# Graph rows for the neighbour table prepared one pass ahead in a pipelined four-layer graph kernel

## The chip, the cores and the metric

The kernel runs on one core of one Trainium2 chip. The metric is the time of one execution on the device in microseconds (us). For the kernel before it is the median of three runs.

## What is computed

Eight graphs of 1024 nodes with 128 features each, and an integer adjacency matrix of 1024 x 1024 for each graph. Four residual layers follow one another:

```
x = x + gnn0(adj, layernorm(x))      # for each node: maximum over the normalised rows of its
                                     # first 25 neighbours, concatenated with its own, matmul, relu
x = x + ffn0(layernorm(x))           # 8 experts, top 2, hidden 512, gelu
x = x + attention(layernorm(x), adj) # 8 heads of 16, masked by the adjacency
x = x + ffn1(layernorm(x))           # router of 64, 6 experts of 128, top 2, three layers, relu
```

The first layer needs rows of arbitrary neighbours: `feats = X[idx]` with X the normalised rows of the whole graph, and then the maximum over them.

## The kernel before

The work of four graphs overlaps. A pass `g` does the attention and the second expert layer of graph g (`att`), prepares the attention of graph g+1 (`unit`), does the graph layer's matmul and the first expert layer of graph g+2 (`near`), and gathers the neighbours of graph g+3 (`load`). The passes -3, -2 and -1 fill this pipeline, passes 0 to 4 are one hardware loop over the same code, and passes 5, 6 and 7 drain it (L586 to L602).

For each pass `planned` (L113) writes down chains of steps and what each step waits for; `schedule` (L250) puts the steps into one list, by a table of assumed durations (`COURSE`). Every engine walks that one list in order and does its own part of each step. So within an engine the order is fixed by the list, and engines wait for one another by semaphores. The steps that matter here:

- `load_x` (SP, L713): the rows of graph g+3 into `xn0`, 512 KB. `lnv(0)` (VectorE, L831 to L836) takes mean and variance, `sq(0)` (ScalarE, L1212) the root, `ln(0)` (VectorE, L850, L852) normalises in place. `store_x` (SP, L723) writes `xn0` to `table` in device memory.
- `load_adj(t)` (SP, L728) brings one of eight row tiles of the adjacency, `deg(t)` (ScalarE, L1196, L1199) counts degrees, `class(t)` (TensorE L1308, ScalarE L1204, L1207) classes the tile, `find(t)` (VectorE, L870 to L886) searches the slot indices.
- The gathers (POOL, L794): 8, 16 or 25 indirect DMAs per tile from `table` into `G`. POOL waits once in a pass for the stored table, then for `find(t)` and for `pmax(t-2)` of each tile. `pmax(t)` (VectorE, L902 to L919) takes the maximum.
- In the next pass `gT` transposes `xn0` and the maxima, `gnn` multiplies, `gnn_add` (VectorE, L930, L933) adds to `res_n`, which `load_res` (SP, L720) has loaded.
- `qT` (ScalarE) copies the transposed rows of the attention input to `XB`; `qk(1)` and `v` (the projections, TensorE) read it. After `v` nothing reads `XB` until the next pass.
- `stack(0)` and `stack(1)` (SP, L748): twelve loads each of query and key parts. `load_mask(t)` (SP, L732), `mask(t)` and `s(t,h)` (TensorE L1408, VectorE L1124): score maxima, 64 a pass.
- `st`, `av` (TensorE L1431, L1434, L1445, ScalarE L1258): attention, in the first third of a pass. `up0`, `down0` (L1386, L1396) and ScalarE's GELU (L1251): first expert layer. `u1`, `u2`, `y1`: second expert layer, after `t1`, `r1`, `lg1` (its router).

SP's queue carries all loads and stores but the gathers. It, too, is walked in order: an SP instruction that waits holds up every transfer behind it.

Of the kernel before, what the change touches and what calls it, by code (L numbers as in the profile page):

```python
# [24 lines left out]
P = 128  # L25
# [87 lines left out]
def planned(att, unit, near, load):  # L113

    p = Plan()
# [4 lines left out]
    if att:  # L120
# [15 lines left out]
        p.gate(("lnv", 3), ("ln", 0) if load else None)  # L136
# [20 lines left out]

    if load:
        p.chain([("load_x",), ("lnv", 0), ("sq", 0), ("ln", 0), ("store_x",)])
        p.gate(("load_x",), ("gT",) if near else None)  # L160
        p.threads.append([("pmax", t) for t in range(TILES)])
        p.threads.append([("gather", t) for t in range(TILES)])
        p.chain([k for t in range(TILES) for k in (("load_adj", t), ("deg", t), ("class", t), ("find", t))])
        p.gate(("find", 0), ("shift",))
        for t in range(TILES):
            p.gate(("gather", t), ("find", t), ("store_x",), ("pmax", t - 2) if t >= 2 else None)
            p.gate(("pmax", t), ("gather", t))
        if not near:
            p.threads.append([("load_w",)])
            p.gate(("load_w",), ("load_adj", 0))  # L170
# [79 lines left out]
def schedule(att, unit, near, load):  # L250


    p = planned(att, unit, near, load)
# [61 lines left out]
def signals(step):  # L315
# [21 lines left out]
    if k == "load_x":  # L337
        return [("xin", step, 16)]
    if k == "store_x":
        return [("tab", step, 16)]  # L340
# [74 lines left out]
class Pass:  # L415


    def __init__(self, before, att, unit, near, load):
        self.att, self.unit, self.near, self.load = att, unit, near, load
        self.steps = schedule(att, unit, near, load)  # L420
# [26 lines left out]
def graph_kernel(nc, x, adj, gW, gb, Wg, bg, W1, b1, W2, b2, Wq, Wk, Wv, Wo, bo,  # L447
                 rw1, rb1, rw2, rb2, ew1, eb1, ew2, eb2, ew3, eb3, out):
    ctx = ExitStack()
    with ctx:  # L450
# [3 lines left out]
        def sem(name):  # L454
# [90 lines left out]
        rden = sb("rden", [P, HTILES, GH])  # L545
        XF = mask[:, TILES - 2:TILES, :].rearrange("p a n -> p (a n)").bitcast(F32)
# [26 lines left out]
            "took": "residual_taken", "resx": "residual_loaded", "tab": "table_stored",  # L573
# [12 lines left out]
        for g in range(-3, GRAPHS):  # L586
            parts_of = (g >= 0, 0 <= g + 1 < GRAPHS, 0 <= g + 2 < GRAPHS, g + 3 < GRAPHS)
            if g > 0 and all(parts_of):
                continue
            passes.append((g, Pass(state, *parts_of)))  # L590
            loops = GRAPHS - 3 if all(parts_of) else 1
            state = passes[-1][1].after(loops)

        def over_passes(eng, body):

            for g, ps in passes:
                if g == 0:
                    with eng.Fori(0, GRAPHS - 3) as b:
                        body(ps, b, b)
                else:  # L600
                    body(ps, 0, g)
# [101 lines left out]
        def _(sp):  # L703
# [3 lines left out]
            def body(ps, turn, b):  # L707
                for step in ps.steps:
                    kind = step[0]
                    if kind == "load_x":  # L710
                        if ps.near:
                            sp.wait_ge(*is_taken(ps, turn, ("xn", 1)))
                        sp.dma_start(xn0[:, :, :], x_v[b + 3, :, :, :]).then_inc(S["xin"], 16)  # L713
# [7 lines left out]
                    elif kind == "store_x":  # L721
                        sp.wait_ge(*at(ps, turn, "xn0", ("ln", 0)))
                        sp.dma_start(table[0:NODES, :].rearrange("(t p) c -> p t c", p=P),  # L723
                                     xn0[:, :, :]).then_inc(S["tab"], 16)
# [39 lines left out]
        def _(pool):  # L764
# [54 lines left out]
        def _(dve):  # L819
# [5 lines left out]
            def moments(ps, turn, i):  # L825
# [3 lines left out]
                src, own = (xn0, res_n, res_b, res_f)[i], (1, 0, 0, 1)[i]  # L829
# [8 lines left out]
            def norm(ps, turn, step):  # L838

                i = step[1]  # L840
                src, dst = ((xn0, xn0), (res_n, xn), (res_b, xn), (res_f, xn))[i]
# [339 lines left out]
        def _(act):  # L1181
# [7 lines left out]
            def body(ps, turn, b):  # L1189
                for step in ps.steps:  # L1190
# [26 lines left out]
                    elif kind == "qT":  # L1217
                        for hf in range(2):
# [67 lines left out]
        def _(pe):  # L1286
# [15 lines left out]
            def body(ps, turn, b):  # L1302
                for step in ps.steps:
# [11 lines left out]
                    elif kind == "gT":  # L1315

                        pe.wait_ge(*at(ps, turn, "xn0"))
# [213 lines left out]
```

## Time and profile before

| what | us |
|---|---|
| median of 3 runs (lowest, highest) | 3047.97 (3043.27, 3052.67) |
| the profiled execution | 3052.26 |
| its span, from the first to the last instruction | 3050.2 |
| TensorE (PE) busy | 2532.1, 83% |
| VectorE (DVE) busy | 1840.7, 60% |
| ScalarE (ACT) busy | 1340.0, 44% |
| POOL busy | 865.5, 28% |
| mean granted TensorE clock | 0.932 |

The engine shares are averages over passes that are limited by different things, so they are read pass by pass. A busy TensorE isn't necessarily at its peak: the ends of its matmuls are modelled. "issue" in a list of waits is time in which an engine waited for nothing that the profile shows.

### The profile page before, as it was taken

To read this page: it belongs to the slowest core of one execution; us is meant where nothing else is said; L and a number is where in the kernel's file an instruction comes from. 1 tells how busy PE (TensorE), PEld (TensorE's weight loads), DVE (VectorE), ACT (ScalarE), POOL (GpSimd) and SP (SyncE) were. 2 spreads that over 40 slices of the span, in tenths; PEclk is the share of its full clock that TensorE was granted. 3 is DMA by queue.
4 is the path that set the end of the run, shared out by engine and by line. 5 is a ranking of instruction groups with operands and counts; after the bars stand their busy time and mean duration, and the time that the engine had idled before them with its cause. 6 is when DMAs were issued, how large, how long until landed. Compare 5 with 4: busy or idle time off the path is not lost.

```text
span 3050.2 us, 48344 instructions
## 1 busy us (share of the span) xinstructions
PE 2532.1 (83%) x16137; PEld 1511.7 (50%) x16137; DVE 1840.7 (60%) x5404; ACT 1340.0 (44%) x1993; POOL 865.5 (28%) x917
## 2 busy tenths in 40 slices
PE   0039559888799989998899889998899999997796
PEld 0026436444466445654466445654566556644253
DVE  5345467874686558764686557865686188318603
ACT  1024224166434653366435653366425553552163
POOL 4737536307500472017400572007500000000000
PEclk9989869889899999999999999999999999998697
DMA  6626666327401372118411483117411120021000
GB/s 148 81 45 82 79 110 82 52 67 107 72 29 44 78 117 37 43 56 111 65 42 41 83 105 41 43 56 128 49 42 36 25 46 28 29 42 36 22 1 7
DMA packets 107565, 183.69 MB, mean 60 GB/s; under 512 B 21471, under 2 KB 57724, under 8 KB 107260
## 3 DMA queue, kind: packets, MB, share of 16 engines
q0 software_dynamic: 25344, 51.96, 19.0%
q1 hardware_dynamic: 81916, 128.08, 15.3%
q8 instruction: 141, 2.31, 0.3%
q14 instruction: 164, 1.34, 0.1%
HBM read 158.59 MB, written 20.97 MB: 59 GB/s over the span
## 4 chain that ended last, share of the span: by engine, by line
PE 37%; DVE 34%; issue 13%; DVEq 6%; ACT 4%; DMA 3%; SPq 2%; ACTq 0%
DVE tmp L1124 14%; PE PY L1396 7%; PE PH L1386 7%; PE PA L1431 5%; PE PA L1434 5%; PE PY L1445 4%; DVE G L902 2%; DMA adj_sb<-in_adj 2%; DVE res_f L1026 2%; PE PA L1408 2%; DVEq L822 2%; ACT HB L1258 2%; DVE res_n L1026 2%; SPq L748 2%; DVE score L870 2%
## 5 line engine op out<-in xcount | busy, mean ns | idle before, releaser
L794 POOL DMA_INDIRECT G<-table,slot_idx x792 | 839.0, 1059 | 262.6 <-issue 258.7
L1124 DVE CUSTOM_DVE_ANT_0 tmp<-PA,mask 128x1024 bf16<-128x1024 f32 x512 | 626.9, 1225 | 34.8 <-issue 34.8
L1258 ACT ACTIVATE HB<-PA 128x1024 f32<-128x1024 f32 x512 | 498.1, 1022 | 328.2 <-PE PA L1434 327.0
L1251 ACT ACTIVATE HB<-PH,bias_T 128x512 f32<-128x512 f32 x512 | 351.4, 687 | 613.3 <-PE PH L1386 613.1
L1386 PE MATMUL PH<-XT,W_sb 128*128 128x512 f32 x1024 | 521.1, 625 | 33.4 <-ACT HB L1251 16.6
L1396 PEld LDWEIGHTS PY<-W_sb,HB 128*128 128x128 f32 x4096 | 504.5, 192 | 68.9 <-issue 38.5
L1396 PE MATMUL PY<-W_sb,HB 128*128 128x128 f32 x4096 | 509.4, 276 | 2.5 <-DVE res_n L1026 2.5
L1431 PE MATMUL PA<-QS,KS 99*128 99x512 bf16 x1024 | 407.1, 398 | 12.0 <-ACT HB L1258 7.6
L1434 PE MATMUL PA<-identb,mask 128*128 128x128 bf16 x4096 | 410.6, 224 | 0.0
L1434 PEld LDWEIGHTS PA<-identb,mask 128*128 128x128 bf16 x4096 | 328.2, 100 | 135.9 <-issue 19.2
L1408 PE MATMUL PA<-KS,QS 96*128 96x512 bf16 x1024 | 335.1, 412 | 54.2 <-DVE MX L1124 46.8
L675 POOL TENSOR_TENSOR pool_pad<-pool_pad 1x1 f32<-1x1 f32 x112 | 23.5, 219 | 1063.6 <-DVE slot_idx L882 912.4
L1386 PEld LDWEIGHTS PH<-XT,W_sb 128*128 128x128 f32 x1024 | 178.4, 196 | 207.8 <-ACT HB L1251 107.6
L1445 PE MATMUL PY<-HB,VS 128*32 128x512 f32 x2048 | 274.7, 608 | 1.9 <-ACT HB L1258 1.9
L671 DVE MEMSET dve_pad<- 1x1 f32 x669 | 39.5, 59 | 363.0 <-DMA G<-table,slot_idx 151.4
L1279 ACT ACTIVATE parts<-PH,bias_T 128x512 f32<-128x512 f32 x192 | 131.9, 687 | 256.0 <-PE PH L1494 161.8
L1408 PEld LDWEIGHTS PA<-KS,QS 96*128 96x128 bf16 x1024 | 88.7, 100 | 285.2 <-DVE MX L1124 140.2
L1026 DVE SCALAR_TENSOR_TENSOR res_n<-PY,wts,res_n 128x128 f32<-128x128 f32 x512 | 144.3, 344 | 119.7 <-PE PY L1396 108.8
L1431 PEld LDWEIGHTS PA<-QS,KS 99*128 99x128 bf16 x1024 | 102.1, 100 | 177.7 <-ACT HB L1258 136.5
L1290 PE MATMUL PH<-ident,xn 128*128 128x128 f32 x256 | 44.5, 320 | 138.3 <-DVE bias_T L1076 67.3
L902 DVE TENSOR_TENSOR G<-G 128x256 f32<-128x256 f32 (+5 forms) x154 | 110.9, 720 | 59.7 <-issue 52.9
L1153 DVE COPY tmp<-PY 128x512 f32<-128x512 f32 x32 | 22.1, 692 | 205.7 <-PE PY L1445 203.5
(163 smaller groups left out, 2388.3 us busy)
## 6 DMA issues: line engine op xcount, KB each, us to landing
adj_sb<-in_adj SPq DMA_DIRECT2D x64, 512.0 KB
adjm<-in_adj SPq DMA_DIRECT2D x64, 512.0 KB
G<-table,slot_idx POOLq DMA_INDIRECT x792
parts_dram<-parts SPq DMA_DIRECT2D x16, 768.0 KB, 3.5
QS<-parts_dram SPq DMA_DIRECT2D x96, 128.0 KB, 5.6
KS<-parts_dram SPq DMA_DIRECT2D x96, 128.0 KB, 7.9
xn<-in_x SPq DMA_DIRECT2D x8, 512.0 KB, 5.3
table<-xn SPq DMA_DIRECT2D x8, 512.0 KB, 4.3
```

Source lines behind the costliest of these rows:

```text
L794: pool.indirect_dma_start(G[:, t % 2, s, :], None, table, bass.IndirectOffsetOnAxis(slot_idx[:, t, s:s + 1], axis=0), bounds_check=ROWS - ...
L902: settle(dve.tensor_tensor(g[:, 0:even, :], g[:, 0:even, :], g[:, even:2 * even, :], ALU.max))
L1026: ins = dve.scalar_tensor_tensor(out=res[:, t, :], in0=psum(ps, key)[:, tt * C:(tt + 1) * C], scalar=wts[layer][:, layer * TILES + t, e:e ...
L1124: ins = dve.tensor_tensor_reduce(out=junk, in0=psum(ps, step)[:, :], in1=mask[:, t, :], scale=1.0, scalar=LOWEST, op0=ALU.add, op1=ALU.max ...
L1251: act.activation(HB[:, i % 2, c, :], psum(ps, step)[:, :], ACT.Gelu, bias=bias_T[:, e * HC + c:e * HC + c + 1]).then_inc(*emptied(ps, step))
L1258: act.activation(HB[:, kc % 2, 2 * pr:2 * pr + 2, :], psum(ps, key)[:, :].rearrange("p (h q) -> p h q", h=2), ACT.Exp, scale=float(D) ** - ...
L1386: pe.matmul(psum(ps, step)[:, :], W1_sb[:, e, c * P:(c + 1) * P], XT[:, half[hf]], start=True, stop=True).then_inc(*filled(ps, step))
L1396: ins = pe.matmul(psum(ps, key)[:, tt * C:(tt + 1) * C], HB[:, i % 2, c, tt * P:(tt + 1) * P], W2_sb[:, e, c, :], start=(c == 0), stop=(c ...
L1408: ins = pe.matmul(psum(ps, step)[:, half[hf]], QS[0:SROWS, h, t * P:(t + 1) * P], KS[0:SROWS, h, half[hf]], start=True, stop=True)
L1431: pe.matmul(o, KS[0:SROWS + PARTS, h, kc * P:(kc + 1) * P], QS[0:SROWS + PARTS, h, half[qh]], start=True, stop=False)
L1434: ins = pe.matmul(o[:, qt * P:(qt + 1) * P], mask[:, qh * HTILES + qt, kc * P:(kc + 1) * P], identb[:, :], start=False, stop=(qt == HTILES ...
L1445: ins = pe.matmul(psum(ps, key)[32 * hh:32 * hh + 32, :], VS[:, kc, (D + 1) * (g * GH + hh):(D + 1) * (g * GH + hh) + 32], HB[:, kc % 2, h ...
```

## The change

A fifth part of a pass, `ahead`, does `load_x`, `lnv(0)`, `sq(0)`, `ln(0)` and `store_x` for graph g+4. The pipeline gets one more pass at its start (-4), and the loop has four passes (0 to 3); pass 4 becomes code of its own. The rows are loaded and normalised in `XB` (under the name `XR`), so `load_x` waits for the projection `v`, and the store waits until the current graph's last maximum is taken and the table has been read. A new step `again` (SP) reads the normalised rows of graph g+3 back from the table into `xn0`, where `load_x` stood. POOL now waits for the table of the preceding pass.

```diff
+    if ahead:
+        p.chain([("load_x",), ("lnv", 0), ("sq", 0), ("ln", 0), ("store_x",)])
+        p.gate(("load_x",), ("v",) if unit else None)
+        p.gate(("lnv", 0), ("ln", 3) if att else None, ("ln", 1) if near else None)
+        p.gate(("store_x",), ("pmax", TILES - 1) if load else None, ("again",) if load else None)
+
     if load:
-        p.chain([("load_x",), ("lnv", 0), ("sq", 0), ("ln", 0), ("store_x",)])
-        p.gate(("load_x",), ("gT",) if near else None)
+        p.threads.append([("again",)])
+        p.gate(("again",), ("gT",) if near else None)
...
         for t in range(TILES):
-            p.gate(("gather", t), ("find", t), ("store_x",), ("pmax", t - 2) if t >= 2 else None)
+            p.gate(("gather", t), ("find", t), ("pmax", t - 2) if t >= 2 else None)
...
-        for g in range(-3, GRAPHS):
-            parts_of = (g >= 0, 0 <= g + 1 < GRAPHS, 0 <= g + 2 < GRAPHS, g + 3 < GRAPHS)
+        for g in range(-4, GRAPHS):
+            parts_of = (g >= 0, 0 <= g + 1 < GRAPHS, 0 <= g + 2 < GRAPHS, 0 <= g + 3 < GRAPHS, g + 4 < GRAPHS)
...
                     if kind == "load_x":
-                        if ps.near:
-                            sp.wait_ge(*is_taken(ps, turn, ("xn", 1)))
-                        sp.dma_start(xn0[:, :, :], x_v[b + 3, :, :, :]).then_inc(S["xin"], 16)
+                        if ps.unit:
+                            sp.wait_ge(*is_taken(ps, turn, ("v", 1)))
+                        sp.dma_start(XR, x_v[b + 4, :, :, :]).then_inc(S["xin"], 16)
+                    elif kind == "again":
+                        stored = settled(sp, at(ps, turn, "tab"))
+                        if ps.near:
+                            seen = settled(sp, is_taken(ps, turn, ("xn", 1)))
+                            sp.wait_ge(*seen)
+                        sp.wait_ge(*stored)
+                        sp.dma_start(xn0[:, :, :], table[0:NODES, :].rearrange("(t p) c -> p t c", p=P)).then_inc(S["xrow"], 16)
...
                 if ps.load:
                     pool.drain()
-                    pool.wait_ge(*at(ps, turn, "tab", ("store_x",)))
+                    pool.wait_ge(*at(ps, turn, "tab"))
...
                     elif kind == "qT":
+                        act.wait_ge(*at(ps, turn, "tab"))
```

In `COURSE` the assumed duration of `load_x` goes from 7 to 14, and `again` gets 6.

The steps of the list move accordingly. SP's queue in the loop pass, from the second half of the stack loads to the adjacency tile 6, of the kernel before:

```order
L748 DMA QS<-parts_dram 16x4x1024 x6
L748 DMA KS<-parts_dram 16x4x1024 x6
L731 REGISTER_ALU
L732 ISA
L732 DMA adjm<-in_adj 128x1024
L727 REGISTER_ALU
L728 ISA
L728 DMA adj_sb<-in_adj 128x1024
```

and of the change:

```order
L772 DMA QS<-parts_dram 16x4x1024 x6
L772 DMA KS<-parts_dram 16x4x1024 x6
L720 REGISTER_ALU
L721 ISA
L721 DMA XB<-in_x 128x8x128
L755 REGISTER_ALU
L756 ISA
L756 DMA adjm<-in_adj 128x1024
L751 REGISTER_ALU
L752 ISA
L752 DMA adj_sb<-in_adj 128x1024
```

The x load (L721) has come in ahead of the mask's adjacency tile and of adjacency tile 6.

VectorE in the same place of the loop pass, from `ln(3)` to the search `find(6)`, of the kernel before:

```order
L850 RECIPROCAL rstd<-sq 128x8
L852 TENSOR_SCALAR xn<-res_f,mv,rstd 128x128 x8
L1023 REGISTER_ALU
L1026 SCALAR_TENSOR_TENSOR res_n<-PY,wts,res_n 128x128 x4
L866 REGISTER_ALU
L671 MEMSET dve_pad 1x1
L868 TENSOR_LOAD degree_class
```

and of the change:

```order
L874 RECIPROCAL rstd<-sq 128x8
L876 TENSOR_SCALAR xn<-res_f,mv,rstd 128x128 x8
L1047 REGISTER_ALU
L1050 SCALAR_TENSOR_TENSOR res_n<-PY,wts,res_n 128x128 x4
L852 REGISTER_ALU
L855 BN_STATS st<-XB 128x6 x8
L858 BN_AGGR mv<-st 128x2 x8
L860 TENSOR_SCALAR sd<-mv 128x8
L890 REGISTER_ALU
L679 MEMSET dve_pad 1x1
L892 TENSOR_LOAD degree_class
```

`lnv(0)` stands ahead of `find(6)` now; its reciprocal and normalisation (`ln(0)`) stand right behind `find(6)`. Of the score maxima L1124 that VectorE did before the router's `sm`, four come later.

ScalarE behind the hole that the profile shows there, of the change (L1236 is the root `sq(0)` with its table load, L1209 are the copies of `t1`; before, the copies followed the GELU L1251 directly):

```order
L1276 ACTIVATE HB<-PH,bias_T 128x512
L1235 REGISTER_ALU
L1236 ACT_TABLE_LOAD
L1236 ACTIVATE sq<-sd 128x8
L1209 ACTIVATE mask<-PH 128x512
```

The next GELU after it needs its table loaded again; in the attention stage a pair of loads around the root is gone, so a pass has as many loads as before.

## Rows read from the trace of the kernel before

**Rows 1.** The page: its first line.

```profile
span 3050.2 us, 48344 instructions
```

**Rows 2.** Busy time by pass: stretch, length, busy us of each engine, clock, DMA share, GB/s.

```profile
187.00:372.00 185.00, 137.64 (x734) 94.21 (x733) 95.25 (x288) 67.59 (x132) 112.79 (x119) 0.86 0.56 69
...
952.00:1290.00 338.00, 308.36 (x2017) 187.71 (x2017) 227.89 (x671) 169.45 (x251) 105.88 (x111) 0.96 0.35 65
```

(The engines are PE, PEld, DVE, ACT and POOL, each with its number of instructions.)

**Rows 3.** Timeline of POOL: its first wait in passes -3, -2 and -1.

```profile
39.17 0.18 POOL L675 TENSOR_TENSOR pool_pad<-pool_pad 1x1 f32<-1x1 f32 x1 [35.60 <-DMA table<-xn]
...
216.38 0.18 POOL L675 TENSOR_TENSOR pool_pad<-pool_pad 1x1 f32<-1x1 f32 x1 [39.84 <-DVE slot_idx L882]
...
421.09 0.18 POOL L675 TENSOR_TENSOR pool_pad<-pool_pad 1x1 f32<-1x1 f32 x1 [58.28 <-DMA table<-xn]
```

**Rows 4.** Waits in pass 1 (952 to 1290): us in total, times, longest.

```profile
POOL pool_pad L675 <- DVE slot_idx L882: 192.6, 1, 192.6
```

**Rows 5.** Busy time by stage of pass 1, columns as in rows 2.

```profile
966.00:1093.00 127.00, 117.22 (x1023) 65.79 (x1024) 72.84 (x222) 89.43 (x126) 53.55 (x54) 0.93 0.45 84
...
1104.00:1124.00 20.00, 10.52 (x50) 6.11 (x49) 8.74 (x36) 9.55 (x17) 10.78 (x15) 0.85 0.72 109
...
1166.00:1259.00 93.00, 90.88 (x456) 56.96 (x455) 80.08 (x212) 31.12 (x46) 2.80 (x3) 1.00 0.16 41
1259.00:1296.00 37.00, 36.65 (x200) 24.47 (x199) 26.20 (x70) 12.12 (x18) 0.00 (x0) 1.00 0.10 35
```

**Rows 6.** Pass 1: a link of the chain that ended last, then TensorE's timeline.

```profile
1104.48 15.23 DMA adj_sb<-in_adj
...
1121.49 0.19 PE L1308 MATMUL PH<-excess,ones 128*1 128x2 f32 x2 [7.67 <-ACT excess L1199]
```

**Rows 7.** The same wait in pass 0, and ScalarE's wait for adjacency in pass 3.

```profile
PE PH L1308 <- ACT excess L1199: 10.7, 1, 10.7
...
  DMA adj_sb<-in_adj: 1.0, 1
```

**Rows 8.** Timeline of VectorE, pass -3: the first statistics.

```profile
16.52 1.64 DVE L831 BATCH_NORM_STATS2 st<-xn 128x6 f32<-128x128 f32 x8
```

**Rows 9.** Timeline of VectorE, pass 1: `lnv(0)`, the next statistics, `ln(0)`.

```profile
982.83 1.65 DVE L831 BATCH_NORM_STATS2 st<-xn 128x6 f32<-128x128 f32 x8 [0.16 <-issue]
...
985.54 1.64 DVE L831 BATCH_NORM_STATS2 st<-res_n 128x6 f32<-128x128 f32 x8
...
1001.84 2.14 DVE L852 TENSOR_SCALAR xn<-xn,mv,rstd 128x128 f32<-128x128 f32 x8
```

**Rows 10.** Timeline of ScalarE, pass 1: table load and root of `sq(0)`.

```profile
999.67 1.28 ACT L1212 ACT_TABLE_LOAD   x1
1000.97 0.21 ACT L1212 ACTIVATE sq<-sd 128x8 f32<-128x8 f32 x1
```

**Rows 11.** The page, DMA issues: KB each, median us from issue to landing.

```profile
xn<-in_x SPq DMA_DIRECT2D x8, 512.0 KB, 5.3
table<-xn SPq DMA_DIRECT2D x8, 512.0 KB, 4.3
```

**Rows 12.** SP's timeline, start of pass 0: first and last of four loads, its landing.

```profile
623.56 0.36 SPq L728 DMA_DIRECT2D adj_sb<-in_adj  x1
...
625.46 0.38 SPq L713 DMA_DIRECT2D xn<-in_x  x1
...
DMA to landing us min/median/max: 7.0/7.0/7.0
```

**Rows 13.** Timeline of VectorE: `find(0)` of pass -2, pass -2's end, `gnn_add` of pass -1.

```profile
205.27 1.23 DVE L870 SCALAR_TENSOR_TENSOR score<-adj_sb,countdown 128x1024 f16<-128x1024 int32 x1 [0.59 <-issue]
...
369.36 0.06 DVE L919 MEMSET dve_pad<- 1x1 f32 x1 [0.29 <-issue]
...
375.87 0.69 DVE L930 TENSOR_TENSOR tmp<-PH,gb_b 128x512 f32<-128x512 f32 x1 [1.31 <-PE PH L1332]
```

**Rows 14.** Timeline of TensorE: its first instruction in pass 1.

```profile
966.48 0.65 PE L1290 MATMUL PH<-ident,xn 128*128 128x128 f32 x4 [2.28 <-issue]
```

More of the change, by code:

```diff
@@ L110, in chain, with planned @@
         return line
-def planned(att, unit, near, load):
+def planned(att, unit, near, load, ahead):
     p = Plan()
@@ L247, with schedule @@
 LATER = {"y0", "y1", "av", "ctx", "proj", "lg0", "lg1", "wT", "gnn", "b", "qk", "mT"}
-def schedule(att, unit, near, load):
-    p = planned(att, unit, near, load)
+def schedule(att, unit, near, load, ahead):
+    p = planned(att, unit, near, load, ahead)
     heads = [0] * len(p.threads)
@@ L415, with __init__ @@
 class Pass:
-    def __init__(self, before, att, unit, near, load):
-        self.att, self.unit, self.near, self.load = att, unit, near, load
-        self.steps = schedule(att, unit, near, load)
+    def __init__(self, before, att, unit, near, load, ahead):
+        self.att, self.unit, self.near, self.load, self.ahead = att, unit, near, load, ahead
+        self.steps = schedule(att, unit, near, load, ahead)
         self.start = dict(before)
@@ L572, in graph_kernel @@
             "xn": "normed_ready", "x1": "gnn_done", "xin": "x_loaded",
[L573 removed]
+            "took": "residual_taken", "xrow": "normed_input_back", "resx": "residual_loaded", "tab": "table_stored",
             "adj": "adjacency_loaded", "adjf": "adjacency_used",
@@ L590, in graph_kernel @@
             passes.append((g, Pass(state, *parts_of)))
-            loops = GRAPHS - 3 if all(parts_of) else 1
+            loops = GRAPHS - 4 if all(parts_of) else 1
             state = passes[-1][1].after(loops)
@@ L597, in over_passes @@
                 if g == 0:
-                    with eng.Fori(0, GRAPHS - 3) as b:
+                    with eng.Fori(0, GRAPHS - 4) as b:
                         body(ps, b, b)
@@ L721, in body @@
                     elif kind == "store_x":
-                        sp.wait_ge(*at(ps, turn, "xn0", ("ln", 0)))
+                        if ps.load:
+                            normed_last = ps.steps.index(("ln", 0)) > ps.steps.index(("pmax", TILES - 1))
+                            again = settled(sp, at(ps, turn, "xrow", ("again",)))
+                            if normed_last:
+                                sp.wait_ge(*at(ps, turn, "xn0", ("ln", 0)))
+                            else:
+                                sp.wait_ge(*at(ps, turn, "aggr", ("pmax", TILES - 1)))
+                            sp.wait_ge(*again)
+                        else:
+                            sp.wait_ge(*at(ps, turn, "xn0", ("ln", 0)))
                         sp.dma_start(table[0:NODES, :].rearrange("(t p) c -> p t c", p=P),
-                                     xn0[:, :, :]).then_inc(S["tab"], 16)
+                                     XR).then_inc(S["tab"], 16)
                     elif kind == "load_adj":
@@ L828, in moments @@
                     dve.wait_ge(*at(ps, turn, "xin", ("load_x",)))
-                src, own = (xn0, res_n, res_b, res_f)[i], (1, 0, 0, 1)[i]
+                src, own = (XR, res_n, res_b, res_f)[i], (1, 0, 0, 1)[i]
                 for t in range(TILES):
```

8 lines of the change are left out of this document (5 added, 3 removed), and 2 rows, old and new, of the table COURSE.

## The prediction

> **What bounds the kernel now.** I read the page first, then busy time by pass, then the waits of one loop pass, then its stages. The span is 3050.2 us [rows 1]. The program is a pipeline of passes: -3 (gathers only), -2, -1, the loop of five passes 0 to 4, and 5 to 7, which gather nothing. Two kinds of pass are bound by different things.
>
> In pass -2 TensorE is busy for 138 of 185 us and POOL, with its gathers, for 113 [rows 2]; its gathers start late, since POOL sat 39.8 us waiting for the first slot indices [rows 3]. Behind the last gather stand two maxima and the next pass, so this pass ends when its gathers do: moving their start moves its end.
>
> In a loop pass TensorE is busy for 308 of 338 us [rows 2], and POOL waits 192.6 us for slot indices [rows 4]: its 106 us of work have room. In the attention stage TensorE is busy 117 of 127 us, VectorE 73, ScalarE 89 [rows 5]. In the late stretch (1166 to 1259) TensorE is busy 90.9 of 93 and VectorE 80: both are nearly full. In the last 37 us VectorE has some 11 to spare. The one hole is between 1104 and 1124, where TensorE works 10.5 of 20 us [rows 5]. There the chain of waits runs through the load of adjacency tile 6: 15.2 us from issue to use, since it stands behind twelve stack loads on SP's queue. ScalarE waits for it, and in order behind that stand the GELUs that TensorE needs; TensorE waits 7.67 us in this pass [rows 6], 10.7 in pass 0, while in pass 3 ScalarE waits for that tile only 1.0 us [rows 7].
>
> Does the table hold the gathers up at all, which the change addresses? Only twice: in pass -3 (released at 39.17) and in pass -1 (421.09); in pass -2, as in the loop, it is the slot indices [rows 3, 4].
>
> **The start (pass -4 new, pass -3).** The table of graph 0 must now be stored before SP goes on. VectorE is free for the first statistics at 16.52 [rows 8]. Statistics take 2.7 us (982.83 to 985.54), the normalisation 2.1 plus a short reciprocal, 2.5 in all [rows 9]; ScalarE's table load and root lie between, 1.28 and 0.21 [rows 10]. The store is issued near 16.5 + 2.7 + 1.5 + 2.5 = 23.2 and lands 4.3 us later [rows 11], at 27.5. Only then do the read-back and adjacency tile 0 go out. Four such loads took 8.9 us (623.56 to 625.46 + 7.0) [rows 12], and one alone 4.3, so each further one costs about 1.5 to 2.2; tile 0 is there near 34. Degree and class take an estimated 3 us (the class matmul runs 1.8 us after a tile has landed, at 1119.7 and 1121.49 [rows 6], and the search another one later). With the search of 11 us (205.27 to 216.38) [rows 3, 13] that gives slot indices near 48 where POOL was released at 39.17: **+9 us**. Bounds 6 and 12.
>
> **Pass -2.** Ahead of the search for tile 0 VectorE did the statistics of the new x (2.7), ln(1) and ln(0) (2.5 each) [rows 9]; now all three come behind it. Gathers start 7.7 us sooner, and the pass ends with them: **-8**. SP is one thing that could spoil it: load_res and adjacency tile 0 now stand behind the store, which waits for the last maximum. Four transfers in 8.9 us [rows 12] arrive just as gnn_add and the search come up, so I count nothing; if the rate is worse, up to +4.
>
> **Pass -1.** The same queue at its start holds store, adjacency, mask adjacency and load_res, where before the middle two had long been loaded. gnn_add started at 375.87; with SP released by the last maximum at 369.4 [rows 13], the four are there near 378.5: **+3**. The x load takes the place of a store of equal size before the same adjacency tile, so it adds nothing here; VectorE's work only changes places. That the gathers may start some 20 us sooner pays nothing: begun at 421 [rows 3] and as long as those of pass -2 (216 to 369), they end near 574, and the pass only near 620 [rows 12].
>
> **The loop, attention stage.** Statistics and normalisation (5.2 us of VectorE), one table store, and on ScalarE a table load for the root plus one back to exp, 2.6 + 0.2 us, go. They lay beside TensorE, which is full here, and VectorE waits for TensorE right after, at the logits. I take **-0.5** in each of five passes (-2.5); bounds 0 and the whole ScalarE piece, 2.8.
>
> **The loop, the hole.** In four passes (0 to 3) the 512 KB x load now stands between the stacks and adjacency tile 6. Its price is not in the trace: at the quiet rate 2.2 us [rows 12], alone to landing 5.3 [rows 11]. The DMA engines are full here and gathers run beside it, so I take 3.5, nearer the middle. It goes straight onto the wait of 10.7, 7.7 and the like [rows 6, 7] in passes 0 to 2, 10.5 in all; in pass 3, with 1.0 of wait, I take 1.5. **+12**. The wait added at issue (for the projection v) is over before the stacks are out.
>
> **The loop, behind the hole.** lnv(0) can run while tile 6 is awaited: free. ln(0), 2.5 us, and the two table switches come after it, on the way to router 1 and the first score maxima; four of the maxima move later. Behind it both engines are near full, but the last 37 us give VectorE 11 to spare [rows 5], and the moved maxima land there, with less expert work left behind them. I take **+1.5** each, +6; bounds 0 and 5.2 + 2.8.
>
> A rule on that: the Trainium skill (ScalarE: Activation LUTs, What ACT_TABLE_LOAD costs) says that a switch takes 1.28 us of load and 1.38 of drain. By that, as an estimate from the page, the pair behind the hole would cost 2.7 us more per pass and the whole change 11 more. The trace has the load at 999.67 and the root at 1000.97 [rows 10]: the load and nothing after it. The rows decide.
>
> **The loop edge.** After each loop pass TensorE waits 2.28 us with nothing to wait for [rows 14]. The loop has four passes now, the fifth being straight code: one edge fewer, **-2**. Pass 4 has no x load at all, which the 4 instead of 5 counts above contain.
>
> **Sum**: 9 - 8 + 3 - 2.5 + 12 + 6 - 2 = +17.5. On the profiled execution's 3052.3 us that is 3069.8; the median of the runs is 4.3 lower, so **3065 us**, 0.6% over it.
>
> **The rivals**, against the median of 3048. A measurement of this kernel tells about 0.3% (9 us) from no change.
>
> *Absorbed (0.27)*: the x load costs 2.2 as in the quiet queue, VectorE's steps fit the slack. 9 - 8 + 3 - 4.5 + 3 x 2.2 = +6: 3054. For it: VectorE idles in the hole too (8.7 busy of 20) [rows 5].
>
> *Faster (0.14)*: ScalarE, not TensorE, ends last in the attention stage, and the moved switches free 2.8 us in each of five passes; tile 6 isn't delayed, since SP's issue of the stacks, not their bytes, sets its arrival. 9 - 8 + 3 - 2 - 14 = -12: 3036. It decides if TensorE's 10 idle us in that stage [rows 5] shrink by more than one per pass. Against it: ScalarE is busy 89 of 127.
>
> *VectorE bound (0.14)*: behind the hole VectorE ends last throughout. Its 5.2, the switches' 2.8 and a load at its full 5.3 add up to 13.3 in four passes: 53 + 4 - 4.5 = +52, 3100. For it: 80 of 93 busy besides the gaps between instructions; against: the slack in the last stretch.
>
> *No earlier gathers (in the forecast, 0.45)*: the change does not do what it says in the loop, because the indices, not the table, start the gathers [rows 4]. That is already counted: it brings nothing there.
>
> **How the numbers follow.** Forecast 0.45, its own range 3055 to 3080 (0.43 of it slower by over 0.3%, 0.02 within). Absorbed 0.27: 0.24 within 0.3%, 0.03 slower. VectorE bound 0.14: slower. Faster 0.14: 0.12 faster by over 0.3%, 0.02 within. That is faster 0.12, same 0.28, slower 0.60. For 8 in 10 the range reaches from 3037, near the faster case's middle, to 3092, which leaves out half of the faster case and most of the VectorE-bound one.
>
> **What would show it.** Pass -3 ends 7 to 11 us later, pass -2 at about the same time as before. POOL's first wait is for slot indices, near 48. In passes 0 to 2 TensorE's wait at the class of tile 6 grows from 8 to 11 us to 11 to 14. The attention stage keeps its length within 1 us. One 2 us wait at a loop edge is gone. I would be wrong if that wait didn't grow, if the attention stage lost 2 us or more, or if the stretch behind the hole grew by more than 4 us per pass.

## The result and the profile after

The changed kernel takes **3083.41 us** (median of 4 runs, 3081.49 to 3089.24) against 3049.95 for the kernel before beside it: ratio 1.0116, 95% interval [1.0094, 1.0138], some 35 us slower by the ratio. The forecast was 3065 (3037 to 3092).

The page of the kernel after: its first line, VectorE's and POOL's busy time, and the two transfers that answer to [rows 11].

```profile
span 3081.0 us, 47928 instructions
...
PE 2529.2 (82%) x16137; PEld 1511.3 (49%) x16137; DVE 1840.1 (60%) x5407; ACT 1339.5 (43%) x1993; POOL 861.5 (28%) x917
...
XB<-in_x SPq DMA_DIRECT2D x8, 512.0 KB, 10.9
table<-XB SPq DMA_DIRECT2D x8, 512.0 KB, 2.9
```

The x load now takes 10.9 us to land instead of 5.3. Where the time went is read from the end of each pass: the moment at which SP issues the first copy of the score maxima (`QS<-mT`). Length of each pass in the two profiled executions, us:

| pass | before, us | after, us | difference | forecast |
|---|---|---|---|---|
| up to the end of -3 | 183.0 | 188.2 | +5.2 | +9 |
| -2 | 186.4 | 180.0 | -6.4 | -8 |
| -1 | 252.0 | 274.5 | **+22.5** | +3 |
| 0, 1, 2, 3 | 328.1, 338.3, 341.0, 346.4 | 333.2, 343.4, 347.8, 350.9 | +21.5 | +16 |
| 4 | 335.4 | 326.3 | -9.1 | -2.5 |
| 5 to 7 | 739.6 | 736.7 | -2.9 | 0 |

(For passes -3 and -2, which copy no maxima, the end is the last pooled maximum.) The sum is the 30.8 us between the two spans.

This mark does not stand at the same place of TensorE's work in both kernels, since four score maxima of a loop pass come later now. At the end of pass 3 it lies 16.4 us ahead of TensorE's first transposes of the next pass before, and 9.1 us after. Counted from one pass's first transposes to the next's, passes 0 to 3 took 345.6, 337.8, 341.3 and 346.0 us before and 345.1, 343.2, 348.0 and 348.6 after: **+14.2**, where the table has +21.5. Pass 4 took 333.5 and 332.1: **-1.4**, where the table has -9.1. The rest to the end is -3.3. The sums up to the end of pass -1 are the same either way. TensorE's first instruction in passes 1 and 2 after, the counterpart of [rows 14]:

```profile
987.27 0.65 PE L1315 MATMUL PH<-ident,xn 128*128 128x128 f32 x4 [2.15 <-issue]
...
1330.51 0.65 PE L1315 MATMUL PH<-ident,xn 128*128 128x128 f32 x4 [2.01 <-issue]
```

POOL's first waits, the counterpart of [rows 3], in its timeline after:

```profile
46.58 0.18 POOL L683 TENSOR_TENSOR pool_pad<-pool_pad 1x1 f32<-1x1 f32 x1 [43.01 <-DVE slot_idx L906]
...
213.26 0.18 POOL L683 TENSOR_TENSOR pool_pad<-pool_pad 1x1 f32<-1x1 f32 x1 [31.29 <-DVE slot_idx L906]
...
395.47 0.18 POOL L683 TENSOR_TENSOR pool_pad<-pool_pad 1x1 f32<-1x1 f32 x1 [33.75 <-DVE slot_idx L906]
```

The change does what it says: none of the three is for the table any more, and in pass -1 the gathers start at 395 instead of 421. Pass -1 is also where most of the time is lost. SP's timeline in pass -1 (start, length, instructions in a row, count), first of the kernel before, then of the kernel after:

```profile
417.44 3.72 SPq L748 DMA_DIRECT2D QS<-parts_dram  x6
421.20 3.29 SPq L748 DMA_DIRECT2D KS<-parts_dram  x6
424.54 2.77 SPq L748 DMA_DIRECT2D QS<-parts_dram  x6
427.35 2.77 SPq L748 DMA_DIRECT2D KS<-parts_dram  x6
430.16 0.42 SPq L728 DMA_DIRECT2D adj_sb<-in_adj  x1
```

```profile
415.45 5.00 SPq L772 DMA_DIRECT2D QS<-parts_dram  x6
420.49 14.55 SPq L772 DMA_DIRECT2D KS<-parts_dram  x6
435.09 2.43 SPq L721 DMA_DIRECT2D XB<-in_x  x1
437.56 13.83 SPq L772 DMA_DIRECT2D QS<-parts_dram  x6
451.44 7.58 SPq L772 DMA_DIRECT2D KS<-parts_dram  x6
459.06 0.42 SPq L752 DMA_DIRECT2D adj_sb<-in_adj  x1
```

The 24 stack loads took SP 13 us; with the x load between them they take 44. Adjacency tile 2, behind them, goes out at 459 instead of 430. TensorE pays twice, in its timeline after:

```profile
444.02 1.04 PE L1433 MATMUL PA<-KS,QS 96*128 96x512 bf16 x2 [20.24 <-DMA KS<-parts_dram]
...
467.17 0.19 PE L1333 MATMUL PH<-excess,ones 128*1 128x2 f32 x2 [15.11 <-ACT excess L1223]
```

Before, the longest waits of these two kinds were:

```profile
PE PH L1308 <- ACT excess L1199: 7.8, 1, 7.8
...
PE PA L1408 <- DMA KS<-parts_dram: 6.0, 1, 6.0
```

The two waits grew by 14.2 and 7.3 us, 21.5 together. Over the whole pass TensorE's idle time grew by 18.8 us (60.2 to 79.0), so other waits got shorter, and its busy time by 3.7 (191.8 to 195.5) at a mean granted clock of 0.79 instead of 0.83. That makes the 22.5.

In the loop, the hole of [rows 6] looks so in pass 1 after (ScalarE's timeline, then TensorE's):

```profile
1144.38 1.06 ACT L1220 ACTIVATE edges<-adj_sb 128x1024 uint8<-128x1024 int32 x1 [13.96 <-DMA adj_sb<-in_adj]
...
1146.09 1.28 ACT L1276 ACT_TABLE_LOAD   x1
1147.39 0.69 ACT L1276 ACTIVATE HB<-PH,bias_T 128x512 f32<-128x512 f32 x1
```

```profile
1146.13 0.19 PE L1333 MATMUL PH<-excess,ones 128*1 128x2 f32 x2 [13.08 <-ACT excess L1223]
```

TensorE's waits of this kind over passes 0 to 3, before and after:

```profile
PE PH L1308 <- ACT excess L1199: 26.6, 3, 10.7
```

```profile
PE PH L1333 <- ACT excess L1223: 43.8, 4, 14.6
```

### The profile page after: what moved, and what is told of

Its sections match the earlier page's. It is cut to its first block, busy times and chain, and to the rows that moved or that the text cites. A ratio compares the mean times of both kernels' runs of the same rounds, so it can differ in the third digit from the quotient of the medians.

```text
span 3081.0 us, 47928 instructions
## 1 busy us (share of the span) xinstructions
PE 2529.2 (82%) x16137; PEld 1511.3 (49%) x16137; DVE 1840.1 (60%) x5407; ACT 1339.5 (43%) x1993; POOL 861.5 (28%) x917
## 4 chain that ended last, share of the span: by engine, by line
PE 48%; DVE 25%; issue 11%; DVEq 5%; ACT 4%; SPq 3%; DMA 3%; ACTq 0%
PE PY L1421 9%; PE PH L1411 9%; DVE tmp L1148 8%; PE PA L1456 5%; PE PY L1470 5%; PE PA L1459 5%; PE PA L1433 4%; SPq L772 3%; DVE G L926 2%; DMA adj_sb<-in_adj 2%; DVEq L846 2%; PE PH L1512 2%; PE PH L1519 2%; PE PY L1527 2%; DVE score L894 2%
## 5 line engine op out<-in xcount | busy, mean ns | idle before, releaser
L1333 PE MATMUL PH<-excess,ones 128*1 128x2 f32 x128 | 12.2, 165 | 184.8 <-ACT excess L1223 183.7
## 6 DMA issues: line engine op xcount, KB each, us to landing
XB<-in_x SPq DMA_DIRECT2D x8, 512.0 KB, 10.9
```

## The experiments

Three theories for pass -1: the early gathers slow the stack loads (theory 1), the x load between the stacks does (theory 2), or the moved order of maxima and searches makes the pass longer whatever the transfers do (theory 3). For the loop: the x load's place, the normalisation behind the hole, the new order, or the loop itself. Each ratio is to the kernel before, run beside it. Two of the experiments (8 and 9) are one and the same kernel, and their ratios are 0.0025 apart, with intervals that do not meet: a difference of 8 us between two experiments is not told from none by the ratios alone. So the lengths of single passes are given too, and they scatter: the unchanged loop code of the kernel after took 1384.9, 1380.9, 1377.7 and 1380.7 us for passes 0 to 3, by TensorE's transposes, in the profiles of after and of experiments 1, 2 and 3. `behind(steps, a, b)` in the edits moves step a right behind step b; the edits stand in `Pass`, after the plan is made, unless another place is shown.

**1. Gathers of pass -1 held until the stacks have landed.**

```diff
                     pool.wait_ge(*at(ps, turn, "tab"))
+                    if ps.unit and not ps.att:
+                        pool.wait_ge(*at(ps, turn, "stack1", ("stack", 1)))
```

> The changed kernel, but in pass -1 alone POOL starts its gathers only when the stacks (0 and 1) have landed. Measured so far: pass -1 took 252.0 us before the change (end of the last maxima's transposes to the same point) and 274.4 after. Theory 1 (the gathers, which now start some 24 us earlier, slow the 24 stack loads from about 0.5 to 2.3 us per issue): SP issues the stack loads at about 0.5 to 0.6 us each again, TensorE's wait for the part of the key stack shrinks from 20 to some 8 us, pass -1 gets 15 to 20 us shorter, the kernel comes to about 3066. Theory 2 (the x load between the two stacks does it): the stack loads stay slow, and pass -1 within 4 us of 274. Theory 3 (the moved order of the maxima and searches makes pass -1 longer, whatever the transfers do): the stacks are fast and the pass is still over 268.

Ratio 1.0112 [1.0088, 1.0136]: no gain. But the loads of the key stack, by tile (duration min/median/max, first and last start), are as theory 1 said, here after and in this run:

```profile
L772 SPq DMA_DIRECT2D KS<-parts_dram x12: 426/1990/3641, 420.5 to 458.6; - x12
```

```profile
L772 SPq DMA_DIRECT2D KS<-parts_dram x12: 426/426/838, 416.8 to 425.4; - x12
```

The first score ran at 427.2 instead of 444.0. Since the order of the steps is that of the kernel after, it is the gathers that slow the issues. But pass -1 took 281.8 us, not the 15 to 20 less that theory 1 expected: quick stacks and a pass over 268 is what was written down for theory 3. VectorE stood at the first maxima, which the list had placed for early gathers (its waits in pass -1):

```profile
DVE dve_pad L679 <- DMA G<-table,slot_idx: 28.4, 2, 23.7
```

POOL was released at 440.07 here, 19 us later than in the kernel before. One wait took the place of another: a hold in the code without one in the plan tests nothing by its time.

**2. In pass -1, the x load behind adjacency tile 2.** `behind(steps, ("load_x",), ("load_adj", 2))`.

> The changed kernel, but in pass -1 alone the x load goes out behind both stacks and behind adjacency tile 2, not between the stacks. Theory 2 (the x load's place in the queue makes pass -1 long): pass -1 falls from 274 to 260 or less. Theory 1 (the early gathers do): the x load's own issue of 2.4 us and its share of the DMA engines move behind the second stack, worth 2 to 4 us and no more; pass -1 at 270 to 272, each stack load's issue still over 2 us.

Ratio 1.0077 [1.0053, 1.0100]. That is 12 us less, but hardly any of it is in pass -1. By its profile the pass ends at 638.5 instead of 642.7, and it began 2.9 us earlier: it took 273.2 us, against 274.5 after, and 272.8, 272.4 and 273.1 in experiments 4, 6 and 17, whose pass -1 is that of the kernel after. The rest of the drop lies in passes whose code is unchanged; what caused it was not found. Theory 2 explains about 1 of the 22 us.

**3. Gathers held until stack 0 has landed, and planned so.** As 1 with `("stack", 0)`, and in `planned`:

```diff
-            p.gate(("gather", t), ("find", t), ("pmax", t - 2) if t >= 2 else None)
+            p.gate(("gather", t), ("find", t), ("pmax", t - 2) if t >= 2 else None,
+                   ("stack", 0) if unit and not att else None)
```

> The changed kernel; in pass -1 POOL starts its gathers when stack 0 has landed, and the plan of that pass counts on it (a gather's gate also names the step stack(0)), so that the maxima stand later in VectorE's order. The first held run showed stack loads back at 0.43 us per issue and the first score at 427 instead of 444, but VectorE then sat 28.4 us ahead of the first maxima, which the unchanged order had placed early. If the early gathers, and only they, are what made pass -1 22 us longer: SP's stack loads quick, VectorE's wait for gathered rows under 6 us, pass -1 at 252 to 260, kernel 3060 to 3070. Rival (pass -1 is long because more stands behind its middle, the statistics, the normalisation and four moved maxima): stacks quick, but pass -1 still over 266, and the tail of scores and maxima at its end longer than before.

Ratio 1.0048 [1.0023, 1.0073], 3055.11: 20 us of the loss gone with this alone. Pass -1 takes 257.1 us instead of 274.5, inside the 252 to 260 expected (the kernel's time is under its 3060 to 3070); in the five kernels below that hold this repair and the x load behind tile 2 (13 to 16 and 18) it takes 251.0 to 255.8, and with the code of the kernel before 249.1 to 255.2 in seven profiles. SP issues the stacks, with the x load between them, in 13 us:

```profile
413.17 2.68 SPq L773 DMA_DIRECT2D QS<-parts_dram  x6
415.89 2.78 SPq L773 DMA_DIRECT2D KS<-parts_dram  x6
418.71 0.43 SPq L722 DMA_DIRECT2D XB<-in_x  x1
419.18 2.92 SPq L773 DMA_DIRECT2D QS<-parts_dram  x6
422.14 4.08 SPq L773 DMA_DIRECT2D KS<-parts_dram  x6
426.27 0.42 SPq L753 DMA_DIRECT2D adj_sb<-in_adj  x1
```

The x load stands where it stood in the slow queue and costs 0.43 us there. POOL was released at 427.31, when all of this had been issued. Theory 1 holds, with one combination not run: early gathers with the maxima in this later order. So how much of the 22.5 us the order alone would cost is not measured; in the profile of after, no wait of VectorE in pass -1 is for gathered rows.

**4. In the loop, the x load behind adjacency tile 6**, and the statistics behind the search for it.

```diff
+        if att and ahead:
+            self.steps = behind(self.steps, ("load_x",), ("load_adj", 6))
+            self.steps = behind(self.steps, ("lnv", 0), ("find", 6))
```

> The changed kernel, but in the loop passes 0 to 3 the x load goes out behind adjacency tile 6 rather than ahead of it, and the new x's statistics come behind the search for tile 6. If the x load ahead of tile 6 is what the hole costs (3.5 us per pass in the forecast): ScalarE's wait for tile 6 goes back from 14 to 15.5 us to 8.5 to 11.5, and each of the passes 0 to 2 gets 3 to 6 us shorter, the kernel about 12 us. Rival (the passes are longer because of VectorE's normalisation and the two table loads behind the hole, or the bytes beside the gathers): the wait shrinks, but the time moves less than 4 us in all, since the statistics now stand behind the search.

Ratio 1.0079 [1.0057, 1.0100]: 11 us less, as expected, though experiment 2 moved the ratio as far without touching the loop. By TensorE's transposes passes 0 to 3 took 1374.4 us, 3 to 11 less than in the four profiles of the unchanged loop. TensorE's wait over these passes is near that before:

```profile
PE PH L1342 <- ACT excess L1232: 28.4, 3, 13.4
```

**5. No x load at all in pass -1 and the loop.** SP's `dma_start(XR, ...)` only where `not ps.unit`; VectorE waits for the projection `v` itself.

> The changed kernel without any x load in pass -1 and the loop passes 0 to 3: the statistics, the normalisation and the store run on what the buffer holds, so graphs 3 to 7 have other rows than the reference's; all other instructions are as they were. It bounds what the load's bytes and its place can cost. Forecast's terms: 3.5 to 5.5 us in each of passes 0 to 2, 1.5 in pass 3; in pass -1 nothing by theory 1 beyond the 2.4 us of its issue, 15 or more by theory 2. Kernel by theory 1 about 3065 to 3068, by theory 2 about 3050.

Graphs 3 to 7 are computed from rows that were not loaded. Ratio 1.0052 [1.0033, 1.0072]: 19 us less, within two of theory 1's range. Pass -1 took 271.5 us, 1 to 3 less than with the load. Passes 0 to 3 took 1374.4 us by TensorE's transposes, as in experiment 4: in the profiles, moving the load brings all that leaving it out does.

**6. The changed kernel without statistics, root and normalisation of the new x in the loop.** The three steps are taken out of the list where `att and ahead`.

> The changed kernel without statistics, root and normalisation of the new x in the loop passes 0 to 3 (the rows loaded there are stored as they came, so graphs 4 to 7 are computed from rows that are not normalised); the x load, the store and the read-back stay. It prices the term behind the hole. Forecast's term: 1.5 us per pass, 6 in all, bounds 0 and 8 per pass. Kernel about 3077 by the forecast; under 3065 if VectorE is the bound behind the hole (over 4.5 per pass).

**7. The kernel before without the same steps in its loop.**

> The kernel before the change without the same three steps in its loop passes 0 to 4 (rows stored as loaded, graphs 3 to 7 are computed from rows that are not normalised). It prices what the attention stage gains when they go. Forecast's term: 0.5 us per pass, bounds 0 and 2.8: kernel 3045 (3034 to 3048). Rival, from pass 4 of the changed kernel, which has no x work and is 9.7 us shorter than before: over 3 us per pass, kernel under 3032.

Experiment 6: 1.0094 [1.0077, 1.0112], 7 us less. The forecast's +6 fits, but so does nothing: the two intervals overlap, and passes 0 to 3 took 1379.1 us by TensorE's transposes, amid the unchanged ones. Experiment 7: 0.9997 [0.9983, 1.0010]: in their old place the steps cost 1 us, not told from none.

**8. and 9. The kernel before with its last loop pass as straight code**, run twice.

```diff
-            if g > 0 and all(parts_of):
+            if 0 < g < GRAPHS - 4 and all(parts_of):
...
-                    with eng.Fori(0, GRAPHS - 3) as b:
+                    with eng.Fori(0, GRAPHS - 4) as b:
```

> The kernel before the change with its fifth loop pass as straight code behind a loop of four, in the same order. It prices the loop edge alone: forecast's term -2 us (2.28 us of TensorE waiting per edge), pass 4 333 instead of 335. Rival: straight code brings more, or costs more where its instructions are fetched for the first time; pass 4 over 337 or under 331.

> The kernel before the change with its last loop pass as straight code once more, beside the others on one chip: 0.9955 again (0.993 to 0.998) if the 13 us belong to the kernel; 0.998 to 1.001 if they were the spread between executions.

Ratios 0.9955 [0.9940, 0.9969] and 0.9980 [0.9971, 0.9989]: 14 and 6 us less for one pass, where the forecast had 2. Little of it is in the pass that was taken out. By TensorE's transposes pass 4 took 332.4 and 329.7 us instead of 333.5, and passes 0 to 3, still in the loop, 1361.1 and 1359.3 instead of 1370.7. So the profiled execution before was a slow one of its kind (3052.26 us, with medians of 3042 to 3050).

**10. Its first loop pass as straight code instead.**

> The kernel before the change with its first loop pass as straight code and the other four in the loop, same order of steps. The last pass as straight code gave a ratio of 0.9955, some 13 us, where the forecast's term for one edge was 2. If one back edge fewer is the cause, this gives the same 0.994 to 0.997. If the gain belongs to what follows the loop (its way out, or the straight code behind it), this stays at 0.998 to 1.001.

Ratio 0.9967 [0.9953, 0.9981], 10 us less: that it matters which pass is taken out is not shown.

**11. First and last as straight code. 12. No loop at all.**

> The kernel before the change with its first and last loop pass as straight code and the middle three in the loop. Two edges fewer: 12 to 25 us and a ratio of 0.992 to 0.996 if each edge costs 6 us or more; 0.996 to 0.998 if the first straight pass brings what there is to have, as one peeled pass did.

> The kernel before the change with all five loop passes as straight code, same order of steps. The forecast priced a back edge at 2 us of TensorE's wait; one pass taken out of the loop measured 6, 10 and 14 us in three comparisons. If a back edge really costs that much: four edges gone bring 25 to 50 us, ratio 0.984 to 0.992, and the 2 us wait for nothing at the start of a pass is gone everywhere. If it costs the 2 us, or if the gain is that of the one way out of the loop: 8 to 15 us, ratio 0.995 to 0.9975.

Ratio 0.9940 [0.9923, 0.9957] with two out, 18 us; **0.9888 [0.9868, 0.9909] with all five out, 3009.06 us** (4 runs within 1.8 us). A pass in the loop costs some 7 us more than the same steps as straight code. VectorE's waits for nothing in passes 0 to 3, the first three and two smaller groups of the kernel before, then of the one without a loop:

```profile
DVE dve_pad L671 <- issue: 39.0, 154, 7.9
DVE G L902 <- issue: 26.9, 32, 1.1
DVE score L870 <- issue: 22.1, 32, 1.0
...
DVE res_f L1026 <- issue: 5.3, 32, 0.2
...
DVE res_n L1026 <- issue: 2.7, 16, 0.2
```

```profile
DVE G L895 <- issue: 27.4, 34, 1.3
DVE score L863 <- issue: 18.3, 32, 0.6
...
DVE dve_pad L664 <- issue: 1.0, 2, 0.5
```

Summed over all groups they are 150.5 and 83.3 us, 17 less per pass; with the same loop code they were 143.2 and 141.2 in experiments 8 and 9, and for the kernel after 130.0 with its loop and 78.6 without, 13 less per pass. L671 is the small memset that stands behind VectorE's waits: 154 pauses there in the loop, 2 without. In the loop each awaited value is worked out from the loop's counter (`turn * count + start`), in straight code it is a constant. That this arithmetic is what the pauses are fits the places where they vanish, but was not tried alone, nor told apart from what else the loop adds (the profile lists 48344 instructions with it and 46115 without).

**13. Three repairs at once**: experiments 2, 3 and 4.

> The changed kernel with three repairs at once: in pass -1 the gathers held until stack 0 has landed and planned so; in pass -1 the x load behind adjacency tile 2; in the loop the x load behind adjacency tile 6 and the statistics behind the search for tile 6. If pass -1's 22 us and the hole are two separate causes that together make the loss, the parts add: 20 (ratio 1.0116 to 1.0048) and 11 (1.0116 to 1.0079), and 2 to 4 for pass -1's own x load, so a ratio of 0.998 to 1.002 to the kernel before (3038 to 3052). If they share a cause, or the normalisation behind the hole is what the loop pays, it stays above 1.003.

Ratio **1.0016 [1.0007, 1.0025]**, 3047.89, inside the expected 0.998 to 1.002. 30 of the 35 us are gone, about the 20 of experiment 3 and the 11 of experiment 4.

**14. The same without the three steps on the new x in the loop.**

> The kernel with three repairs without statistics, root and normalisation of the new x in the loop passes 0 to 3 (graphs 4 to 7 are computed from rows that are not normalised). With the hole repaired it prices those three steps once more: removed from the changed kernel they gave 1.0094 for 1.0116, 7 us, with an interval that holds 1 to 13. The forecast's +1.5 per pass: 6 us less, ratio 0.9996. If they are the whole rest of the loop's loss: 10 us or more, under 0.9985. If nothing: within 0.001 of 1.0016.

Ratio 1.0008 [0.9998, 1.0018], 2 us less: the case written down for "nothing" (within 0.001 of 1.0016), not the 6 of the forecast. Together with experiment 6, the steps behind the hole cost 0 to 7 us in all four passes, and no run tells that from nothing.

**15. Three repairs, the x work still later in the loop.**

```diff
+            self.steps = behind(self.steps, ("load_x",), ("load_adj", 7))
+            self.steps = behind(self.steps, ("lnv", 0), ("pmax", 7))
+            self.steps = behind(self.steps, ("sq", 0), ("lnv", 0))
+            self.steps = behind(self.steps, ("ln", 0), ("acc1", 5))
+            self.steps = behind(self.steps, ("store_x",), ("ln", 0))
```

> As the kernel with three repairs, but in the loop the x load goes behind adjacency tile 7 and statistics, root, normalisation and store of the new x behind the last pooled maximum, amid the second router's experts. Forecast's term behind the hole (1.5 us per pass for VectorE's 5.2 and the switches where router 1 waits): the way to router 1 is free of them, 4 to 8 us less than the kernel with three repairs in all. Rival (they cost the same wherever they stand, since both engines are full up to the end of the pass): within 3 us of it.

Ratio 1.0129 [1.0112, 1.0147], 34 us slower than experiment 13: both expectations miss. The statistics now come right ahead of the root, and ScalarE, which works in order, stands there until VectorE is through; behind it wait the relus of router 1's experts (L1321, `parts`). ScalarE's wait in passes 0 to 3, with three repairs and then here, and TensorE's wait that is new here:

```profile
ACT sq L1250 <- DVE sd L874: 6.4, 4, 2.9
```

```profile
ACT sq L1253 <- DVE sd L877: 25.6, 4, 7.4
...
PE PH L1529 <- ACT parts L1321: 24.9, 4, 7.3
```

So here the place of these steps is worth far more than what they take.

**16. Three repairs, the rest of the loop in the order before the change.** The planner runs with the old gates for the loop, and the x work is placed by hand.

> The kernel with three repairs (ratio 1.0016), but its loop passes keep the order of steps that they had before the change (the planner run with the old gates, then the x load placed behind adjacency tile 6, the statistics behind the search for tile 6, the root behind the first down-product of the second half-tile, the normalisation behind t1, the store behind the last maximum, the read-back where the x load was). Passes 0 to 3 of the kernel with three repairs take 1363 us, those before 1354 (profile before) to 1344. If the planner's new order (four maxima later, more of them at the end) costs the rest: passes 0 to 3 at 1345 to 1355 and a ratio of 0.993 to 0.998. Rival (the x work and its bytes cost it there, whatever the order of the rest): 1360 to 1366, ratio 1.000 to 1.003.

Ratio 1.0036 [1.0022, 1.0049], outside both expected ranges: the new order is not at fault, since the old one is no faster (6 us slower here by the ratios).

**17. The changed kernel, and 18. the one with three repairs, without a loop.**

> The changed kernel with every pass as straight code. The kernel before without its loop has a ratio of 0.9888 (3009 against 3042): 34 us for five passes, some 7 each, most of it VectorE's pauses for nothing, 150.5 us in passes 0 to 3 and 83.3 without the loop. If the cost belongs to each pass in the loop, the changed kernel, whose loop has four, gains 27 (ratio 1.0116 to 1.0027), and stands 43 us above the loopless kernel before: the change's own price with the loop taken out of the comparison. If the loop hid what the moved work costs, or the straight code makes VectorE's work behind the hole free: under 1.000.

> The kernel with three repairs (ratio 1.0016), every pass as straight code. By 7 us for each of four loop passes: ratio 0.992 to 0.994 (3019 to 3025), 8 to 16 us above the loopless kernel before. Rival (the rest of the loop's loss is VectorE's pauses, which the loop makes and which only hurt where the x work stands behind the hole): 0.990 or less, within 4 us of the loopless kernel before.

Ratio 1.0032 [1.0022, 1.0042] for the first, as expected: some 44 us above the loopless kernel before (1.0032 / 0.9888). The second has 0.9962 [0.9949, 0.9975], 23 above it and outside both expected ranges: 16 us less than with its loop, where 23 to 29 were expected. In its profile, taken in the slowest of six executions (3045.39, median 3034.28), TensorE's waits at the degree class are back, though the x load stands behind tile 6:

```profile
PE PH L1340 <- ACT excess L1230: 41.4, 3, 15.2
```

Its pass 1 issues adjacency tile 6 at 1103.64, 14.7 us behind the first load of stack 1 (1088.98), against 11.1 in experiment 13. So moving the x load does not always repair the hole; what lengthens the issues of the stacks there stays open.

## Why the prediction was wrong

The direction was right and the size half: +17.5 forecast, +30.8 in the profile, +35 by the ratio. Stretch by stretch, pass -1 is off by 19.5 us and every other one by less than 4. Step by step:

- **The start: +9, measured +5.2.** Right. POOL was released at 46.6, forecast 48, 7.4 us later than before, and the pass ended 5.2 us later. That is a little under the lower bound of 6, but in the other profiles this end comes at 180.5 to 183.0 with the old code and at 187.7 to 189.8 with the new.
- **Pass -2: -8, measured -6.4.** Right.
- **Pass -1: +3, measured +22.5. This is the step that failed**, in the sentence "That the gathers may start some 20 us sooner pays nothing". It asked what earlier gathers bring and not what they meet. They ran into the 24 stack loads, which before had finished issuing just as the gathers got going. SP's issues of the key stack went from 0.43 to 2 us each, and TensorE waited for the key stack and for tile 2, 21.5 us longer. Experiments 1 and 3 show it: held back, the issues are quick again, and held and planned the kernel gets 20 us back, 17 of them in this pass. That the x load "adds nothing here" was right within 3 us (experiments 2 and 5).
- **The attention stage: -2.5.** From its first transposes to the first load of stack 1 it took 127.1, 126.4, 128.7, 128.8 and 125.5 us in passes 0 to 4; now 124.0, 124.9, 126.5, 127.3 and 126.6. That is 7 us, inside the bounds, but experiment 7 says that at most a few reach the pass's end. The forecast would count itself wrong if the stage lost 2 us or more: it did in passes 0 (3.1) and 2 (2.2).
- **The hole: +12, measured +17.2 in TensorE's waits (26.6 to 43.8).** Moving the load gives 11 us by the ratio and 3 to 11 in the profiled loop passes. Right in place and, within that spread, in size. I called the DMA engines full there, where [rows 5] have a share of 0.72, and priced the load by its bytes; but other issues slow as well: in pass 1 that of the mask adjacency took 3.59 us after, 2.05 before. As a whole, passes 0 to 3 got 14.2 us longer, forecast 16.
- **Behind the hole: +6, measured 7 and 2, neither told from nothing.** Inside the bounds. By the rule that adds a drain to each table load (the Trainium skill, ScalarE: Activation LUTs, What ACT_TABLE_LOAD costs) it would be, as an estimate from the page, 11 more. The trace of after decides as that of before did: load at 1146.09 for 1.28, GELU at 1147.39.
- **The loop edge: -2, measured -6 to -14 by the ratios, -1 to -4 in pass 4 itself.** I took one visible wait of 2.28 us at TensorE's first instruction [rows 14] for the whole price. The price is spread over the pass, mostly on VectorE. It may have hidden a part of the loss: without any loop the change costs 44 us.
- **Not accounted for**: with three repairs the kernel is still 5 us slower by the ratio. Passes 0 to 3 take 1363.4 us against 1353.8 before by SP's mark, but 7.3 of these 9.6 us are the mark's shift: by TensorE's transposes it is 1373.0 against 1370.7, or against 1361.1 and 1359.3 in experiments 8 and 9. Neither the order (16) nor the loop (18) explains what is left of it.

Of the rivals, "absorbed" and "faster" are refuted by the hole's growth. "VectorE bound" (3100) lay as near to the time as the forecast, but by luck: VectorE's steps and the switches cost 0 to 7 us, where it has 32 (5.2 + 2.8 in four passes).

## What to carry to other kernels

Taking away the wait that held back a burst of indirect DMAs moves the burst: look at what runs on the queues in the stretch that it moves into, and price that, even if an earlier start itself pays nothing. A hold for such a burst must stand in the plan too, or in-order engines wait for what the plan thought early. Compare a loop pass with a straight one over its whole length: here dropping the loop from the kernel before (0.9888) brought 34 us, about what the change lost. And measure passes between marks that keep their place in the work of the engine that bounds them: a mark that shifts moves time from one pass to the next.

## What was not expected of the hardware

- **SP's issue of a 128 KB load in pass -1 took 0.43 us (median) with few or no gathers beside it and 1.99 us (median, up to 3.64) beside indirect DMAs from POOL**, while its time to landing fell from 13.7 to 4.7 us (medians of the key stack): the wait moved from behind the issue into it, so the next instruction on SP starts later, whatever it is. This fits the Trainium skill (Perfetto Trace Analysis, DMA Instruction — HWDGE (DVE, Sync)), where the bar of such an instruction covers the making of descriptors and can reach into their execution when the buffer is full. That the buffer was full here, no run shows.
- A pass inside the hardware loop cost 7 us more than the same steps as straight code (34 us for five, 26 for the four of the kernel after). The loop is not what makes executions differ: those of the kernel before without it lay within 1.8 us of each other (four runs), but those of the kernel after without it within 17.8 (12 runs), against 16 us for the kernel before (11 runs).
- Gathers beside it are not enough for a slow issue. In pass 1 of the kernel after, POOL was busy for 5.05 of the 6 us from 1084 to 1090, and the twelve loads of stack 0 went out there in 5.5 us, as quickly as ever. What decides between the two cases was not tested. SP's timeline:

```profile
1084.06 2.68 SPq L772 DMA_DIRECT2D QS<-parts_dram  x6
1086.79 2.77 SPq L772 DMA_DIRECT2D KS<-parts_dram  x6
```
